# Gate logits of a DLRM expert kernel: from float32r halves between the expert products to plain float32 products over four column groups

## The reference

```
gates = softmax(einsum('btd,tdk->btk', x[:, :T, :], Gw) + Gb)
task_out = einsum('btk,btkh->bth', gates, sel_eo)
gs = softmax(x[:, T, :] @ Gsw + Gsb);  shared_out = einsum('be,beh->bh', gs, eo)
```

## Time and profile before

| | us |
|---|---|
| median of 3 runs | 2026.48 (2026.4 to 2028.73) |
| the profiled execution | 2026.6 |
| its span | 2024.6 |
| PE busy in it | 2009.0 (99%) |
| DVE busy | 1373.9 (68%) |
| ACT busy | 713.9 (35%) |

### The profile page before, as it was taken

The page is one execution under the profiler, slowest core; times in us unless marked ns, Lnnn a source line. Parts: engine busy times, 40 slices in busy tenths (PEclk is TensorE's granted clock), DMA queues, the critical chain, the costliest instruction groups (busy, mean ns, idle before and its releaser), DMA issues.

```text
span 2024.6 us, 25896 instructions
## 1 busy us (share of the span) xinstructions
PE 2009.0 (99%) x8832; PEld 1640.7 (81%) x8832; DVE 1373.9 (68%) x1429; ACT 713.9 (35%) x962; POOL 170.2 (8%) x152
## 2 busy tenths in 40 slices
PE   8999999999999999999999999999999999999999
PEld 6888788887888888888888788888878888888887
DVE  4488988896266656657555888898943667656564
ACT  3233333333333333332434333323233333423333
POOL 4631000000030002022033000000000000000000
DMA  6543324333343334343344324233323323233331
GB/s 207 174 153 108 124 83 135 101 115 99 94 146 96 113 100 139 104 136 116 102 136 135 125 83 136 94 116 123 97 95 93 115 88 121 94 115 93 115 93 42
DMA packets 70007, 230.50 MB, mean 114 GB/s; under 512 B 12398, under 2 KB 12654, under 8 KB 69948
## 3 DMA queue, kind: packets, MB, share of 16 engines
q1 hardware_dynamic: 61688, 208.75, 32.7%
q0 software_dynamic: 7488, 20.98, 3.2%
q10 hardware_dynamic: 772, 0.09, 0.0%
HBM read 229.56 MB, written 0.23 MB: 113 GB/s over the span
## 4 chain that ended last, share of the span: by engine, by line
PE 97%; DVE 1%; issue 1%; ACT 0%; DMA 0%; DVEq 0%; ACTq 0%
PE main L337 28%; PE main L338 28%; PE main L339 28%; PE top L338 3%; PE top L339 3%; PE top L337 3%; PE gps L373 2%; PE gps L371 2%; DVE w_lo L805 0%; DVE act_lo L817 0%; DMA eo_sh<-in_tbl,idx 0%; DVE prod L880 0%; ACT w_hi L494 0%; DVE slots L886 0%; ACT act_hi L513 0%
## 5 line engine op out<-in xcount | busy, mean ns | idle before, releaser
L337 PE MATMUL main<-act_hi,w_hi 128*128 128x512 f32 x2568 | 1001.3, 390 | 4.8 <-DVE act_lo L817 2.8
L338 PE MATMUL main<-act_lo,w_hi 128*128 128x512 f32 x2568 | 1000.2, 389 | 0.0
L339 PE MATMUL main<-act_hi,w_lo 128*128 128x512 f32 x2568 | 1000.1, 389 | 0.0
L805 DVE TENSOR_TENSOR w_lo<-raw,w_hi 128x1024 fp32r<-128x1024 f32 (+1 forms) x356 | 433.1, 1217 | 600.5 <-ACT w_hi L494 575.8
L494 ACT ACTIVATE w_hi<-raw 128x1024 fp32r<-128x1024 f32 (+1 forms) x356 | 375.5, 1055 | 1101.8 <-PE main L339 993.4
L337 PEld LDWEIGHTS main<-act_hi,w_hi 128*128 128x128 f32 x2568 | 482.1, 188 | 118.5 <-issue 7.4
L339 PEld LDWEIGHTS main<-act_hi,w_lo 128*128 128x128 f32 x2568 | 482.2, 188 | 100.5
L338 PEld LDWEIGHTS main<-act_lo,w_hi 128*128 128x128 f32 x2568 | 482.1, 188 | 99.8
L886 DVE TENSOR_TENSOR slots<-slots,prod 128x1024 f32<-128x1024 f32 (+2 forms) x202 | 245.1, 1213 | 6.0
L328 POOL DMA_INDIRECT slots<-in_tbl,idx x144 | 166.1, 1153 | 918.3 <-DVE act_lo L817 612.2
L880 DVE TENSOR_TENSOR prod<-eo_sh,gate_b 128x1024 f32<-128x1024 f32 x136 | 165.6, 1218 | 1.9
(11 more groups left out here) (65 smaller groups left out, 570.0 us busy)
## 6 DMA issues: line engine op xcount, KB each, us to landing
raw<-in_w SPq DMA_DIRECT2D x304, 512.0 KB
gate_b<-gates_dram SPq DMA_DIRECT2D x34, 512.0 KB
raw<-in_w_top SPq DMA_DIRECT2D x32, 512.0 KB
raw<-in_w_first SPq DMA_DIRECT2D x16, 512.0 KB
gate_b<-gates_dram SPq DMA_DIRECT2D x16, 256.0 KB
slots<-in_tbl,idx POOLq DMA_INDIRECT x144
raw<-in_w_top SPq DMA_DIRECT2D x4, 256.0 KB
eo_b<-in_dense SPq DMA_DIRECT2D x2, 192.0 KB, 2.8
```

Source lines behind the costliest of these rows:

```text
L337: nc.tensor.matmul(dst, lhs_hi, rhs_hi, start=start, stop=False)
L338: nc.tensor.matmul(dst, lhs_hi, rhs_lo, start=False, stop=False)
L339: return nc.tensor.matmul(dst, lhs_lo, rhs_hi, start=False, stop=stop)
L805: nc.vector.tensor_tensor(w_lo[0:parts, slot, 0:cols], raw[0:parts, rawslot, 0:cols], w_hi[0:parts, slot, 0:cols], ALU.subtract).then_inc( ...
```

## The change

The logits become plain float32 products in one block between unit 0 and unit 1 of a gated step. The eight k are dealt over four groups of 32 output columns of the array: k = 4r + c goes to partitions 32c to 32c + 31 of `gps[0]`, so each group sums two k. The stationary operand is 128 x 32 float32 (n columns, the rest zeros from the host), the moving operand is the float32 activation in `slots` (in the very first step, where it isn't there, act_hi and act_lo in two calls each). DVE transposes all 128 partitions of the bank into `gps[1]` and adds the bias and the four groups' parts. `split_gates`, `gw_raw` and ACT's copy of the logits are gone; SP loads `gw` directly, 128 x 256 float32 each time (before 128 x 32, or 128 x 80 for the shared gate), once logit_done tells that the last logits are done. ACT waits for logit_done before it empties unit 0's bank, since that writes into `slots`. On PE the loops over tasks are written out, the inner loop over units stays.

```diff
-            def logits(Q, behind=0, then=None):
...
+            def logits(Q, x):
+                pe.wait_ge(gw_in, Q * 16 + 16)
+                if not isinstance(Q, int) or Q:
+                    pe.wait_ge(logit_evac, Q)
+                sets = x(0)
+                for r in range(KT // QUADS):
+                    for c in range(QUADS):
+                        k = r * QUADS + c
+                        for n, strip in enumerate(x(k)):
+                            dst = gps[0][c * QUAD:(c + 1) * QUAD, :]
+                            mm = nc.tensor.matmul(as_subs(dst) if len(strip.shape) == 3 else dst, gw[:, k, :], strip,
+                                                  start=(r == 0 and n == 0),
+                                                  stop=(r == KT // QUADS - 1 and n == len(sets) - 1))
+                mm.then_inc(logit_done, 1)
+            def from_halves(k):
+                return [act_hi[:, k, :].bitcast(f32), act_lo[:, k, :].bitcast(f32)]
+            def from_rows(chunk):
+                return lambda k: [x_strip(chunk, k)]
+            def from_slots(chunk):
+                return lambda k: [slots[:, chunk + k, :]]
...
                 expert(0, U, E, S=S, between=between, order=order)
+                if gate:
+                    logits(*gate)
                 expert(1, U + 1, E + 1)
...
                     act.wait_ge(unit_done, U + j)
                     split_hi((j + 1) % 2, (off + j + 1) % RAW, V + (off + j + 1) // RAW)
                     dest_wait(dest, j - 1)
+                    if j == 1 and gates:
+                        act.wait_ge(logit_done, gates[0] + 1)
                     evacuate(main[(j - 1) % 2][:, :], dest(j - 1), bias(j - 1))
...
+            parts = gps[1][:, :].rearrange("p (c i) -> p c i", i=GCOL)
-                after(link(nc.vector.transpose(flat, logit_t[:, :])))
-                after(link(nc.vector.tensor_tensor(lg[:, :, t], turned[:, :, t], turned[:, :, n:2 * n], ALU.add)))
+                dve.wait_ge(logit_done, Q + 1)
+                nc.vector.transpose(gps[1][:, :], gps[0][:, :]).then_inc(logit_evac, 1)
+                dve.wait_ge(logit_evac, Q + 1)
+                bias = gbias[:, bass.ds(col, 1), t].broadcast_to([GCOL, blocks, n])
+                after(link(nc.vector.tensor_tensor(lg[:, :, t], bias, parts[0:QUAD, :, t], ALU.add)))
+                for q in range(1, QUADS):
+                    after(link(nc.vector.tensor_tensor(lg[:, :, t], lg[:, :, t], parts[q * QUAD:(q + 1) * QUAD, :, t],
+                                                       ALU.add)))
```

More of the change, by code:

```diff
@@ L394, in plain_step @@
+            def from_halves(k):
[4 more added lines that the diff above has]
+                return lambda k: [slots[:, chunk + k, :]]
+            def plain_step(U, E, S, between=None, dense_of=None, order=range(KT), gate=None):
                 expert(0, U, E, S=S, between=between, order=order)
+                if gate:
+                    logits(*gate)
@@ L413, in dense_sums, with gated_step, emit @@
                 return emit
-            def gated_step(U, E, S, Q, behind=0, then=None, order=range(KT)):
-                plain_step(U, E, S, between=logits(Q, behind, then), order=order)
+            def gated_step(U, E, S, Q, x, then=None, order=range(KT)):
+                def emit(i, k):
+                    if i == KT - 2:
+                        then()
+                plain_step(U, E, S, between=emit if then else None, order=order, gate=(Q, x))
             def tower(U, S, stop=False):
@@ L461, in _ @@
                 (first, u0), (sf, s0), e0, q0 = places(h), steps(h), h * EUNITS, h * GATED
-                gated_step(first, e0, sf, q0, behind=0 if h else 1)
+                gated_step(first, e0, sf, q0, from_rows(T * KT) if h else from_halves)
                 if h:
                     tower2(h - 1, first + STEP, s0, top)
-                    gated_step(u0 + U_T0, e0 + STEP, s0 + 1, q0 + 1, then=lambda: tower3(h - 1, top[2]), order=AFTER_T2)
-                else:
-                    gated_step(u0 + U_T0, e0 + STEP, s0 + 1, q0 + 1)
-                with pe.Fori(1, T) as t:
-                    gated_step(u0 + U_T0 + t * STEP, e0 + STEP + t * STEP, s0 + 1 + t, q0 + 1 + t)
+                    gated_step(u0 + U_T0, e0 + STEP, s0 + 1, q0 + 1, from_rows(0), then=lambda: tower3(h - 1, top[2]),
+                               order=AFTER_T2)
+                else:
+                    gated_step(u0 + U_T0, e0 + STEP, s0 + 1, q0 + 1, from_rows(0))
+                for t in range(1, T):
+                    gated_step(u0 + U_T0 + t * STEP, e0 + STEP + t * STEP, s0 + 1 + t, q0 + 1 + t, from_rows(t * KT))
                 u, e = u0 + U_SH1, e0 + (T + 1) * STEP
@@ L473, in _ @@
                 e, s, q = e + STEP, s0 + T + 2, q0 + T + 1
-                gated_step(u0 + U_T1, e, s, q)
+                gated_step(u0 + U_T1, e, s, q, from_slots(0))
                 e, s, q, u = e + STEP, s + 1, q + 1, u0 + U_T1N
-                with pe.Fori(0, T - 2) as t:
-                    gated_step(u + t * (STEP + MT1), e + t * STEP, s + t * 2, q + t)
+                for t in range(T - 2):
+                    gated_step(u + t * (STEP + MT1), e + t * STEP, s + t * 2, q + t, from_slots((t + 1) * KT))
                     tower(u + STEP + t * (STEP + MT1), s + 1 + t * 2)
@@ L513, in hand_over, with gate_slot @@
                     nc.scalar.activation(dst, src, ACT.Copy).then_inc(act_hi_rdy, 1)
[L515 to L525, removed]
+            def gate_slot(Q, n):
+                act.wait_ge(shift_rdy, Q + 1)
+                nc.scalar.activation(lg[:, :, 0:n], lg[:, :, 0:n], ACT.Exp).then_inc(exp_rdy, 1)
             def step(U, V, off, dest, bias, gates=None, dense_of=None, y_of=None):
                 for j in range(1, STEP - 1):
-                    if j == 1 and gates:
-                        gate_slot(0, *gates)
                     act.wait_ge(unit_done, U + j)
@@ L714, in _ @@
                 dest, bias = shared_dest({0: [(pair_done, p0)]} if h else {}), biases(bias0, 0)
-                step(first, first // RAW, first % RAW, dest, bias, (q0, 2 * NE, 0))
+                step(first, first // RAW, first % RAW, dest, bias, (q0, NE))
                 first_step_out(h, first + STEP, dest, bias, s0 + 1)
@@ L721, in task0 @@
                     dest, bias = task_dest(t, S, Pb), biases(bias0, STEP + t * STEP)
[L722 removed]
+                    step(U, V, off, dest, bias, (q0 + 1 + t, NG), y_of=y_of)
                     change(U + STEP, V + STEP // RAW, off, dest, bias, S + 1, (t + 1) * KT, shared=shared,
@@ L739, in _ @@
                 dest, bias = task_dest(0, S, Pb), biases(bias1, STEP)
-                step(U, V, off, dest, bias, (Q, 2 * NG, T + 1))
+                step(U, V, off, dest, bias, (Q, NG))
                 change(U + STEP, V + STEP // RAW, off, dest, bias, S + 1, KT)
@@ L749, in task1 @@
                     dest, bias = task_dest(t, Sn, Pn), biases(bias1, STEP + t * STEP)
-                    step(Ut, Vt, off, dest, bias, (Q + 1 + n, 2 * NG, T + 2 + n))
+                    step(Ut, Vt, off, dest, bias, (Q + 1 + n, NG))
                     change(Ut + STEP, Vt + STEP // RAW, off, dest, bias, Sn + 1, (t - 1) * KT)
@@ L964, in run, with step @@
                     op()
-            def step(U, V, off, ops=None, gates=None, split=None, plan=None, late=(), x={}, dense_of=None):
+            def step(U, V, off, ops=None, gates=None, plan=None, late=(), x={}, dense_of=None):
                 queue = []
@@ L1080, in _ @@
                 ops = gating("shared", 4, e0, q0, h, p0)
-                step(first, first // RAW, first % RAW, ops, (q0, NE), (q0 + 1, NG), x=turns[h]["A"])
+                step(first, first // RAW, first % RAW, ops, (q0, NE, 0), x=turns[h]["A"])
                 U = first + STEP
@@ L1129, in _ @@
                     begun = loop_links(n, LINKS_L1)
-                    task1(n, (Q + 2 + n, NG))
+                    task1(n)
                 end_links(begun, T - 2, LINKS_L1)
                 more = h + 1 < HALVES
-                task1(T - 2, ((h + 1) * GATED, NE) if more else None, last=True)
+                task1(T - 2, last=True)
                 U = Un + (T - 1) * both
@@ L1180, in bias_rows, with quad_cols @@
     def bias_rows(v):
-        return np.concatenate([v, np.zeros(GCOL - v.size, np.float32)])
+        return np.concatenate([v, np.zeros(NE - v.size, np.float32)])
+    def quad_cols(w):
+        return kt_cols(np.concatenate([w, np.zeros((D, QUAD - w.shape[1]), np.float32)], axis=1))
     by_table = a["ids"].T
```

67 lines of the change are left out of this document (27 added, 40 removed).

## The result

| | before | after |
|---|---|---|
| median, us | 2027.24 of 4 runs (2026.4 to 2028.73) | 2009.66 of 4 runs (2009.08 to 2010.21) |
| profiled execution, its span | 2026.6, 2024.6 | 2009.13, 2007.1 |

The ratio is 0.9913 [0.9898, 0.9928]: faster by 17.6 us, where 12.4 were forecast (2014.1, range 2005 to 2044). The direction and the mechanism were right, the size was too small by some 5 us.

What follows compares the result with a forecast made beforehand. PE was taken to bound the kernel (busy 2009.0 of 2024.6 us, 97% of the chain of waits). Terms -13.5 + 0.75 + 0.3 = -12.4 from 2026.5 gave 2014.1 us, range 2005 to 2044.

Steps and rivals of the forecast that it cites:

- PE is paid in full: What PE does counts fully in the time, unless PE then arrives somewhere before another engine is ready.
- loose steps: 11 gated steps where DVE has w_lo of unit 2 ready before PE; forecast to gain 1.23 us each, 13.5 in all.
- The block of 2.5 us: New logit matmuls between units 0 and 1 on PE, four groups at once: about 2.5 us a step where 3.73 was spent.
- switch: PE's cost of going from one kind of matmul to the other and back: 0.3 us a block.
- stagger: Late start of the fourth group behind seven weight loads: up to 0.75 us, taken as 0.45 a block.
- (a): Rival: matmuls start in order, so only pairs overlap; block 4.4 us, time 2041, chance 0.20.
- (b): Rival: the column groups don't overlap at all; block 7.4 us, +72, time 2098, chance 0.12.
- (c): Rival: groups overlap but each record waits for its own late-loaded weights; block 3.6 us, time 2027, no change, chance 0.16.
- Tight steps: Six layer 0 steps (tasks 1 to 3, either half), DVE last at unit 2 by 0.17 us: block's gain becomes wait, 0.
- The first half's task 1 by +0.75: Layer 0 step with two row transposes in DVE's way: PE's wait of 0.81 us grows by 0.75.
- The first step by +0.3: Very first step, sixteen calls on the activation halves: its block takes 4.2 us, making the step 0.3 worse.
- Costed at nothing: Side effects on ACT, DVE, SP, gate weight loads, hand-over and written-out loops, taken as covered by other waits: 0 us.

Runs made afterwards that it cites:

- one_group: The changed kernel with all eight k of the logits in one column group, DVE adding zeros for the other parts: 2093.83 us, 1.0328.
- held_back: The changed kernel with the last four of DVE's eight gating operations held back until behind w_lo of the next step's unit 3: 2000.54 us, 0.9867.
- held_back_two: The changed kernel with only the last two of DVE's eight gating operations held back: 1998.68 us, 0.9862.
- six_adds: The changed kernel with three more adds of zeros in DVE's gate chain: 2016.84 us, 0.9949.
- before_written_out: The kernel before the change with its two PE loops over tasks written out, nothing else: 2026.39 us, 0.9996.
- before_held_back: The kernel before the change with the last four of DVE's eight gating operations held back until behind w_lo of unit 3: 2028.25 us, 1.0006.
- turns_late: The changed kernel with two gating operations held back and four row transposes of the first half's task 1 moved behind units 14 and 15: 1997.92 us, 0.985.

## Why the prediction was right, and by how much it was off

- *PE is paid in full.* Held. Each of the 11 loose steps got shorter by what PE saved in it; where DVE was last, none did.
- *The block of 2.5 us.* This is the term that was mis-sized. It was put as 1.72 of slots, 0.3 of switch and 0.45 of stagger. The slots are exact (four bursts 0.43 apart), and the switch is as in tower3: 0.32, 0.52 and 0.34. Going over to column groups and back costs nothing beyond that, which the prediction had left open. The stagger is some 0.03. I had let seven weight loads of 0.11 go one after another and hid only part of them; the trace has eight within 0.16 us. 1.72 + 0.3 + 0.03 is 2.05, the rows give 2.06. A loose step shows 1.63 of gain where 3.73 - 2.06 gives 1.67; the other 0.04 are in unit 1. Behind its first two matmuls the next ten distances from start to start are 224 to 240 ns, in all 0.06 above the usual 227 each; behind the old logits it was 0.01. At 11 steps the term is worth 17.9 - 13.5 = 4.4 of the 5.1 us of error in the spans; most of the rest is the earlier start of unit 0, below, which is luck.
- *Rivals (a), (b), (c).* All three fall by the block: 4.4, 7.4 and 3.6 us were named, 1.95 came. (b)'s block stands in one_group, 7.07, and that kernel takes 2093.83, where (b) gave 2098 for 7.4. That records start in order, which spoke for (a), is not so between groups.
- *Tight steps gain nothing.* Held to 0.03 us a step. PE is at unit 2 at 13.0 instead of the forecast 13.4, and so waits longer, 1.62 in the rows where 1.3 was named. held_back and held_back_two show that the eight gating operations are the cause.
- *The first half's task 1 by +0.75.* It was +0.90, the size by which the gate chain grew: from w_lo of unit 2 to w_lo of unit 3 it is 306.36 - 301.15 = 5.21, and 306.76 - 302.46 = 4.30 before. The three adds are 0.72 of it; the transpose is 731 ns instead of 693 and starts 1.25 instead of 1.14 after w_lo. The second PE wait is 1.71 (forecast 1.6). In the other tight steps w_lo of unit 3 is there 0.55 ahead of PE (forecast 0.6), and six_adds shows by +0.35 for 0.75 more that this room is about right.
- *The first step by +0.3.* It was +0.10. Its last matmul of unit 0 is at 19.94 and unit 1 starts at 23.86, so the block is 23.86 - (19.94 + 0.23) = 3.7 instead of 4.2, the stagger again.
- *Costed at nothing.* ACT's wait for logit_done, the gate weights' loads and the written-out loops cost nothing that a step shows. No wait for act_lo appeared in unit 0 of a gated step behind a hand-over, which would have been a sign against the prediction: the hand-over feeds it fast enough. PE's waits for act_lo (2.8 us in 2 times, as before) are those of the two ungated steps, and unit 0 of the very first step waits 0.74 in both kernels.
- *Not forecast.* Unit 0 of the first step starts 0.69 us earlier, with the first rows' DMA. It is scatter and not the change: over all profiled executions it starts between 14.59 and 16.47 in the kernel after and those made from it, and between 14.96 and 16.17 in the kernel before and those made from it.
- *PE's idle time* up by 8 to 9 us was named, 10.3 came; busy time down by some 20 was named, 27.8 came, both because the block is shorter.

## What to carry to other kernels

Products with few output columns can be dealt over the array's column groups, and then a slot of the array's time carries four of them: the price is the slots and the switch, with next to nothing for each group. Issue them round by round, or a group with more than four records holds up the others. Before such a gain is booked, look at each step for the engine that arrives last: where it is already on time to 0.2 us, as in a third of the steps here, the gain turns into a wait until that engine's own queue is put in another order.

## What the runs showed of the hardware that was not expected

- Four column groups run plain float32 products fully side by side (16 records in four bursts 0.43 apart). Issued group after group, four records of one group are taken in (one runs, three wait).
- Weight loads of 32 columns for different groups are issued 7 ns apart and overlap, each 106 to 110 ns long.
- The clock fell in some executions in a step of layer 1 that has no gate block, after PE had stood still for two short waits. PE of before_written_out:

```profile
1481.36 0.47 PE L337 MATMUL main<-act_hi,w_hi 128*128 128x512 f32 x1 [1.42 <-DVE act_lo L817]
...
1482.49 0.48 PE L337 MATMUL main<-act_hi,w_hi 128*128 128x512 f32 x1 [0.21 <-DVE w_lo L805]
...
1484.05 0.63 PE L338 MATMUL main<-act_lo,w_hi 128*128 128x512 f32 x1
1484.48 0.63 PE L339 MATMUL main<-act_hi,w_lo 128*128 128x512 f32 x1
```

The same stretch by windows (window in us, length, busy us of PE, PEld, DVE, ACT and POOL with counts, granted clock, DMA share, GB/s):

```profile
1478.00:1482.00 4.00, 2.58 (x12) 1.76 (x10) 3.27 (x5) 1.35 (x2) 0.00 (x0) 1.00 0.00 0
1482.00:1486.00 4.00, 3.79 (x11) 2.82 (x10) 1.57 (x2) 1.63 (x2) 0.00 (x0) 0.60 0.55 138
1486.00:1490.00 4.00, 4.00 (x18) 3.23 (x18) 0.00 (x0) 0.14 (x1) 0.00 (x0) 0.97 0.41 128
```

For some 3.4 us the matmuls start 0.43 apart instead of 0.23: the granted clock, 0.60 as the mean of the middle window, which holds some of either, is at the lower of its levels, 1.2 GHz instead of 2.4. It costs 1.6 us. The profiles of before and after don't have it; those of before_written_out, before_held_back, six_adds (twice) and turns_late do. The waits are there in the others too (1.43 and 0.20 at 476.17 and 477.31 in the kernel after, where the matmuls from the second one after the wait on start 0.23 to 0.24 apart), so what decides it from one execution to the next is open. It explains part of the scatter of 2 to 3 us among the runs of one kernel (of the eleven of before_written_out this one took 2029.19 at a mean clock of 0.999, the others 2025.94 to 2027.55 at 1.0), and is why the experiments are read by steps first.
